# A fused two-layer network: dummy products moved to the front, GpSimd normalizing and rounding rows, and a new order of all steps

## The reference, cut to what matters

```
x = x + attn0(layernorm(x), ctx)        # 16 heads of 8, softmax
x = x + ffn0(layernorm(x))              # 8 experts of 512, one per row, gelu
x = x + attn1(layernorm(x), ctx)        # 16 query heads, 8 key heads
x = x + ffn1(layernorm(x))              # 15 experts of 128, top 3, and a shared one, relu
```

```
xn = x * rsqrt(mean(x*x) + 1e-6)
scale = 127 / max(max|xn|, 1e-5)
xq = clip(round(xn * scale), -128, 127) / scale
```

## Time and profile before

| | |
|---|---|
| times of three runs | 245.34, 240.26, 245.23 us (median 245.23) |
| profiled execution | 240.89 us, span 239.1 us |
| mean granted clock of TensorE | 0.971 |
| busy PE, DVE, ACT, POOL | 204.0, 174.3, 136.7, 76.7 us |

### The profile page before, as it was taken

How to read it: one execution, slowest core, us unless ns; L and a number is a source line. 1 busy time by engine, 2 the same in 40 slices (tenths; PEclk the granted TensorE clock), 3 DMA queues, 4 the chain that set the end, 5 groups by cost and what they waited for, 6 DMA issues and landing times.

```text
span 239.1 us, 5122 instructions
## 1 busy us (share of the span) xinstructions
PE 204.0 (85%) x1775; PEld 108.0 (45%) x1775; DVE 174.3 (73%) x500; ACT 136.7 (57%) x290; POOL 76.7 (32%) x162
## 2 busy tenths in 40 slices
PE   1687898799989999988478998899989698989994
PEld 1242253234343344567224474333343244889993
DVE  6979779976999566235726648988987832997774
ACT  2622137778849779340269566647777586544651
POOL 8889976992266600011200005400011010201000
PEclk9997589999999999999799999999999999999999
DMA  6152162494002100000003000850000000000000
GB/s 184 30 138 70 44 160 98 58 344 157 3 20 68 44 26 3 0 3 0 0 18 99 25 0 3 248 151 23 0 3 0 2 4 0 3 0 0 26 0 22
DMA packets 12810, 12.42 MB, mean 52 GB/s; under 512 B 2755, under 2 KB 11177, under 8 KB 12785
## 3 DMA queue, kind: packets, MB, share of 16 engines
q0 software_dynamic: 2528, 6.63, 9.8%
q1 hardware_dynamic: 8800, 4.95, 7.5%
q10 hardware_dynamic: 1456, 0.53, 0.9%
HBM read 7.84 MB, written 0.26 MB: 34 GB/s over the span
## 4 chain that ended last, share of the span: by engine, by line
PE 67%; DVE 14%; ACT 9%; issue 4%; DMA 2%; ACTq 1%; POOL 1%; SPq 1%; DVEq 0%; POOLq 0%
PE OB L1504 11%; PE SA L1472 8%; PE SB L1489 7%; ACT prob L836 6%; DVE mx L1086 5%; PE X L1624 3%; PE X L1606 3%; PE SA L1672 3%; PE X L1426 3%; PE X L1613 2%; DMA Q<-nm 2%; PE X L1513 2%; PE SB L1665 2%; PE X L1636 2%; PE SA L1665 2%
## 5 line engine op out<-in xcount | busy, mean ns | idle before, releaser
L1086 DVE TENSOR_REDUCE mx<-SA 128x1 bf16<-128x512 f32 x128 | 80.7, 683 | 14.7 <-PE SA L1472 13.9
L836 ACT ACTIVATE prob<-SB 128x512 f32<-128x512 f32 x128 | 69.4, 595 | 20.2 <-PE SB L1489 19.3
L640 POOL TENSOR_SCALAR vareps<-mv 128x2 f32<-128x2 f32 x10 | 1.9, 191 | 114.1 <-DVE mv L981 114.0
L1504 PE MATMUL OB<-prob,V 128*32 128x256 f32 x512 | 37.6, 387 | 0.3
L1489 PE MATMUL SB<-Q,K 64*128 64x256 bf16 x208 | 28.1, 274 | 3.3 <-ACT prob L836 1.5
L1472 PE MATMUL SA<-K,Q 64*128 64x512 bf16 x104 | 25.4, 388 | 4.3 <-DVE mx L1086 4.3
L1489 PEld LDWEIGHTS SB<-Q,K 64*128 64x128 bf16 x208 | 9.6, 94 | 23.7 <-ACT prob L836 15.6
L1504 PEld LDWEIGHTS OB<-prob,V 128*32 128x32 f32 x512 | 12.5, 108 | 14.1 <-issue 8.9
L1472 PEld LDWEIGHTS SA<-K,Q 64*128 64x128 bf16 x104 | 6.9, 94 | 17.1 <-DVE mx L1086 12.5
L887 ACT ACTIVATE wq<-w0s 128x1024 f32 x8 | 7.8, 1044 | 9.5 <-DVE eid L1238 9.3
L1313 DVE SCALAR_TENSOR_TENSOR acc<-SA,cw,acc 128x128 f32<-128x128 f32 x30 | 8.4, 345 | 1.6 <-PE SA L1672 1.6
(11 more groups left out here) (340 smaller groups left out, 400.2 us busy)
## 6 DMA issues: line engine op xcount, KB each, us to landing
w0s<-in_L_ffn_w_dram POOLq DMA_DIRECT2D x16, 256.0 KB, 4.5
wq<-in_L_ffn_eW_dram POOLq DMA_DIRECT2D x2, 960.0 KB, 7.2
K<-kp SPq DMA_DIRECT2D x12, 128.0 KB, 2.5
Q<-qp SPq DMA_DIRECT2D x18, 64.0 KB, 2.1
Q<-nm SPq DMA_DIRECT2D x50, 0.5 KB
K<-kp SPq DMA_DIRECT2D x12, 64.0 KB, 2.1
cx<-in_ctx_dram SPq DMA_DIRECT2D x2, 256.0 KB, 3.7
Q<-qp ACTq DMA_DIRECT2D x6, 64.0 KB, 2.1
```

The costliest lines, as they stand in the source:

```text
L836: act.activation(prob[:, g % 2, 2 * (i % 2) + a, 2 * u:2 * u + 2, :].rearrange("p k q -> p (k q)"), SB[n % NSB][:, :], ACT.Exp).then_inc(s ...
L1086: dve.tensor_reduce(mx[:, g % 2, i // 2, r, a:a + 1], SA[n % NSA][:, :], AX, ALU.max, negate=True).then_inc(s_sa_max, 1)
L1504: last = pe.matmul(OB[32 * j:32 * j + 32, 0:NQ], V[n][:, b, kt, first:first + 32], prob[:, gg % 2, j, kt, :], start=(kt == 0), stop=(kt == ...
```

## The change

Five things are done at once.

1. A new step `warm` makes two products of 256 columns out of the cleared tile `mx` into bank `OB`. Eight such steps stand at the start of TensorE's queue, two before the first scores. Of the 16 `unread` steps 12 are left.
2. `gnorm`: GpSimd normalizes the heads' output of batch 0 in layer 1 (6 operations on 128x128), in place of VectorE.
3. `round`: GpSimd rounds two of the four quantized tiles (batch 1 of `q1`, batch 0 of `o1`; 4 operations each). VectorE still works out the scales.
4. The casts of the second parts of keys and queries of batch 1, layer 0, go to ScalarE.
5. All steps stand in a new order. The sum over the weights of layer 1 is a step of its own (`w1_sum`).

```diff
+NORM_ON_GPSIMD = ('norm', 'o1', 0)
+ROUND_ON_GPSIMD = [('quant', 'q1', 1), ('quant', 'o1', 0)]
+CAST_ON_SCALAR = [('kproj', 0, 1), ('qproj', 0, 1)]
+SCHEDULE = [('warm', 0), ('zeros', 0), ('zeros', 1), ('warm', 1), ('warm', 2), ('warm', 3), ('stats', 'q0', 0),
...
+                elif kind == "gnorm":
+                    b = step[1]
+                    pool.wait_ge(in_gb, 48)
+                    pool.wait_ge(s_rstd, nth("stats", "o1", b))
+                    for r in range(R):
+                        last = pool.tensor_scalar(hn[:, b, r, :], stage_in["o1"][:, b, r, :], mv[:, b, r, 0:1], rstd[:, b, r:r + 1],
+                                                  ALU.subtract, ALU.mult)
+                    then(last)
+                    for r in range(R):
+                        last = pool.tensor_tensor(hn[:, b, r, :], hn[:, b, r, :], gamma_b[:, :], ALU.mult)
+                    then(last)
+                    for r in range(R):
+                        last = pool.tensor_tensor(hn[:, b, r, :], hn[:, b, r, :], beta_b[:, :], ALU.add)
+                    last.then_inc(s_gnorm, 1)
+                elif kind == "round":
+                    _, stage, b = step
+                    pool.wait_ge(s_scales, quantized_before("quant", stage, b))
+                    for r in range(R):
+                        last = pool.tensor_scalar(hn[:, b, r, :], hn[:, b, r, :], qs[:, b, r:r + 1], MAGIC, ALU.mult, ALU.add)
+                    then(last)
+                    for r in range(R):
+                        last = pool.tensor_scalar(hn[:, b, r, :], hn[:, b, r, :], -MAGIC, dq[:, b, r:r + 1], ALU.add, ALU.mult)
+                    last.then_inc(s_round, 1)
...
+                    if step in CAST_ON_SCALAR:
+                        act.wait_ge(*xread(*step))
+                        act.activation(kp[0:rows, part_buffer(step), 1, :], kr[0:rows, part_buffer(step), :], ACT.Copy).then_inc(s_kp[n][b], 1)
...
+                    if step == NORM_ON_GPSIMD:
+                        act.wait_ge(s_gnorm, 1)
+                    else:
+                        act.wait_ge(s_norm, normed_before(*step))
...
+                    if step == NORM_ON_GPSIMD:
+                        dve.wait_ge(s_gnorm, 1)
+                        then(dve.tensor_reduce(amax[:, b, :], hn[:, b, :, :], AX, ALU.max, apply_absolute_value=True))
+                        continue
...
+                    if step in ROUND_ON_GPSIMD:
+                        dve.scalar_tensor_tensor(qs[:, b, :], inv[:, :], 127.0, rms[:, b, :], ALU.mult, ALU.mult).then_inc(s_scales, 1)
+                        continue
...
+                elif kind == "warm":
+                    pe.wait_ge(s_mx, 1)
+                    for k in range(2):
+                        pe.matmul(OB[:, 0:NQ], mx[:, 0].rearrange("p x r c -> p (x r c)"), mx[:, :].rearrange("p g x r c -> p (g x r c)"),
+                                  start=True, stop=True)
```

More of the change, by code:

```diff
@@ L200, in nth, with normed_before, quantized_before @@
     return ORDER[step[0]].index(step) + 1
+def normed_before(*step):
+    return sum(s != NORM_ON_GPSIMD for s in ORDER["norm"][:nth(*step)])
+def quantized_before(*step):
+    return sum((s in ROUND_ON_GPSIMD) == (step in ROUND_ON_GPSIMD) for s in ORDER["quant"][:nth(*step)])
 def transformer(nc, x, ctx, Wq, bq, Wk, bk, Wv, bv, Wo, bo, w_red, wg, w1, b1, w2, b2, wq1, wk1, wv1, wo1,
@@ L253, in transformer @@
         inv = sb("inv", [P, R])
-        qs = sb("qs", [P, R])
-        dq = sb("dq", [P, R])
+        qs = sb("qs", [P, B, R])
+        dq = sb("dq", [P, B, R])
         cx = sb("cx", [P, B * KT, D])
@@ L806, in _ @@
                     last.then_inc(s_qp[n][b], 1)
+                    if step in CAST_ON_SCALAR:
+                        act.wait_ge(*xread(*step))
+                        act.activation(qp[:, part_buffer(step), 1, :], qr[:, part_buffer(step), :], ACT.Copy).then_inc(s_qp[n][b], 1)
                 elif kind == "kplace":
@@ L852, in _ @@
                     b = step[2]
-                    act.wait_ge(s_norm, nth(*step))
+                    if step == NORM_ON_GPSIMD:
+                        act.wait_ge(s_gnorm, 1)
+                    else:
+                        act.wait_ge(s_norm, normed_before(*step))
                     for r in range(R):
@@ L1006, in _ @@
                         continue
-                    dve.wait_ge(s_norm, nth(*step))
+                    dve.wait_ge(s_norm, normed_before(*step))
                     then(dve.tensor_reduce(amax[:, b, :], hn[:, b, :, :], AX, ALU.max, apply_absolute_value=True))
@@ L1015, in _ @@
                     then(dve.reciprocal(inv[:, :], mxn[:, :]))
-                    dve.tensor_scalar(dq[:, :], mxn[:, :], 1.0 / 127.0, None, ALU.mult)
-                    then(dve.scalar_tensor_tensor(qs[:, :], inv[:, :], 127.0, rms[:, b, :], ALU.mult, ALU.mult))
+                    dve.tensor_scalar(dq[:, b, :], mxn[:, :], 1.0 / 127.0, None, ALU.mult)
+                    if step in ROUND_ON_GPSIMD:
+                        dve.scalar_tensor_tensor(qs[:, b, :], inv[:, :], 127.0, rms[:, b, :], ALU.mult, ALU.mult).then_inc(s_scales, 1)
+                        continue
+                    then(dve.scalar_tensor_tensor(qs[:, b, :], inv[:, :], 127.0, rms[:, b, :], ALU.mult, ALU.mult))
                     for r in range(R):
-                        last = dve.tensor_scalar(hn[:, b, r, :], hn[:, b, r, :], qs[:, r:r + 1], MAGIC, ALU.mult, ALU.add)
+                        last = dve.tensor_scalar(hn[:, b, r, :], hn[:, b, r, :], qs[:, b, r:r + 1], MAGIC, ALU.mult, ALU.add)
                     then(last)
                     for r in range(R):
-                        last = dve.tensor_scalar(hn[:, b, r, :], hn[:, b, r, :], -MAGIC, dq[:, r:r + 1], ALU.add, ALU.mult)
+                        last = dve.tensor_scalar(hn[:, b, r, :], hn[:, b, r, :], -MAGIC, dq[:, b, r:r + 1], ALU.add, ALU.mult)
                     last.then_inc(s_quant, 1)
@@ L1071, in _ @@
                     last.then_inc(xdone(step), 1)
-                    dve.wait_ge(*xread(*step))
-                    dve.tensor_copy(parts[:, 1, :], rest).then_inc(done, 1)
+                    if step not in CAST_ON_SCALAR:
+                        dve.wait_ge(*xread(*step))
+                        dve.tensor_copy(parts[:, 1, :], rest).then_inc(done, 1)
                     dve.wait_ge(done, 2)
@@ L1115, in _ @@
                     dve.tensor_scalar(wgn[:, :], wgn[:, :], wgs[:, 2:3], None, ALU.mult).then_inc(s_wgn, 1)
-                elif kind == "w1_measure":
+                elif kind == "w1_sum":
                     dve.wait_ge(in_w1n, 64)
                     dve.tensor_reduce(wsum[:, :], w1n[:, :, :], AX, ALU.add, apply_absolute_value=True).then_inc(s_wabs, 1)
+                elif kind == "w1_measure":
                     dve.wait_ge(*xfull(step))
@@ L1520, in _ @@
                     else:
-                        pe.wait_ge(s_quant, nth("quant", "o1", b))
+                        pe.wait_ge(s_round if ("quant", "o1", b) in ROUND_ON_GPSIMD else s_quant, quantized_before("quant", "o1", b))
                     for r in range(R):
```

108 lines of the change are left out of this document (55 added, 53 removed), and 54 rows, old and new, of the table SCHEDULE.

## The result

The changed kernel took 245.88 us in the median of four runs (245.19 to 246.62), the kernel before 243.51 in the median of its four (240.26 to 245.34). The ratio is 1.020, with a 95% interval of 1.011 to 1.029. The forecast was 237.7 us, with 233 to 243 as its range; the change is slower by 1 to 2%. Every kernel here has some executions a few us longer at a lower clock (two of the four of the kernel before), and the ratios and the medians of the experiments leave those out.

A forecast was written before the change was run, and what follows sets the result against it. TensorE was taken as the bound (busy 204.0 of 239.1 us, 67% of the chain). From 240.9 us, -0.4 (front), -1.0 and -0.5 (unread products), -1.6 (VectorE's work) and +0.3 (GpSimd's chain) gave 237.7 us, range 233 to 243.

The forecast's parts named there:

- the sentence on the roundings: Roundings moved to GpSimd: 4 operations, 1.6 us, claimed to be covered by over 4 us of steps before their transposes.
- the second attention: Layer 1's attention: fewer unread products and less VectorE work, with GpSimd's slower chain against them; -2.3 us.
- between the layers: Middle of the kernel, where TensorE waits for VectorE: removing a copy or a faster gather brings nothing; 0, ends -1 and +1.
- the last network: End of the kernel: its only pair of unread products removed, all taken as on the path; -0.5 us.
- The front: Start to group 2's exponentials: first reduction at 19.4 (fast) or 21.1 us (slow); net -0.4 us, or +1.3 if slow.
- my third rival: Front: the 16 products end too early and the clock stays at 1.2 GHz past 31 us; 244.0 us, chance 0.12.
- VectorE's relief: Second layer: rounding and normalizing taken from VectorE, 3.6 us of work, half of TensorE's 3.3 us waits returning; -1.6 us.
- GpSimd's chain of six operations: Layer 1, batch 0 normalizing on GpSimd: 2.4 us after a power of 0.7, making ScalarE's squares wait; +0.3 us.
- Unread products: Two pairs dropped in the second attention, one in the last network, all taken as on the path; -1.0 and -0.5 us.
- Nothing of it is on the path: Rival: unread products stood in waits and VectorE's freed time lies idle, only the front counts; 240.5 us, chance 0.20.
- The signs: Trace marks named beforehand, such as first reduction near 19.4 us, clock above 0.9 in 24 to 30 us, VectorE busy 170.5 us.
- GpSimd holds VectorE: Rival: the 14 new GpSimd operations (5.8 us) block VectorE through the shared port, half on the path; 240.6 us, chance 0.06.

The follow-up runs named there:

- round_back: Changed kernel with the rounding of batch 1 of q1 back on VectorE, so the layer 1 weight load issues earlier; 242.7 us, ratio 1.012.
- load_late: Changed kernel with the load of layer 1's expert weights held until the first two maxima of group 13 are done; 241.7 us, ratio 1.003.
- late_max2: load_late with group 2's maxima transposed after the first quarter of group 3 and batch 1's query stacking one place earlier on SyncE's queue; 239.8 us, ratio 0.995.
- late_gap: load_late with GpSimd's fill of V moved later and 24 more products in TensorE's idle gap at the front; 239.8 us, ratio 0.999.
- combo: Changed kernel with the edits of load_late, late_gap and late_max2 together; 238.6 us (3 runs), ratio 0.995.
- combo_sync: combo with the layer 1 expert-weight load on SyncE's queue, issued after the first maximum of group 14; 238.2 us, ratio 0.988.
- after_again: The changed kernel unaltered, measured once more in five later runs; 246.5 us, ratio 1.010.
- no_warm: Changed kernel without its ten new steps of products on the cleared tile; 246.8 us, ratio 1.027.
- sync_unread: combo_sync with three pairs of unread products put back, two in the second attention and one in the last network; 238.9 us, ratio 0.993.
- fill_later: Changed kernel with GpSimd's fill of V moved behind the power of the context's deviation; 245.8 us, ratio 1.010.
- before_load_late: Kernel before with one added wait: layer 1's expert-weight load issues only when all maxima of group 10 are reduced; 245.0 us (2 runs).

## Why the prediction was wrong, point by point

- **The step that failed** is the sentence on the roundings: "The roundings (4 operations, 1.6 us) are covered by over 4 us of steps before their transposes." It is true of the transposes. I did not ask what else stood behind these operations on GpSimd's queue. It was the load of layer 1's weights, and behind that, by way of the shared transfer engines (busy share 1.01 in 156 to 162 us), group 10's maxima. It cost 3.8 to 4.8 us by the medians of round_back and load_late, and 4.1 us of the second attention (62.3 us against load_late's 58.2). I had the price in hand (a move of 4.59 us beside expert loads), but tied it to a slow front alone.
- **The account.** Against the forecast's span of 235.9 us (239.1 and the sum's -3.2) the trace had 244.9, 9.0 more. From the rows of both chains: layer 0 +1.2 where I had -0.4, between the layers -0.1 where I had 0, the second attention +4.1 where I had -2.3, the last network +0.6 where I had -0.5. The second attention's 6.4 us are 4.2 of idle time (TensorE was idle 2.9 us more than before, where I had 1.3 less; the stall alone is 4.08) and 2.2 of busy time (1.2 more, where I had 1.0 less). The clock accounts for the busy part: it was 0.72 in 162 to 168 us, behind the stall, 0.80 in 180 to 186 and 0.92 in 186 to 192 us, and 1.00 in 148 to 204 us before; late_max2, at 1.00 throughout, is busy for 49.8 us of this stretch, 1.4 less than the kernel before. With the load out of the way the stretch takes 57.0 to 58.2 us (load_late, late_gap, late_max2, combo, combo_sync) against 58.2 before, so of the 2.3 us that I had forecast for it 0 to 1.2 us came.
- **The front.** The sum gave 19.4 (fast) or 21.1 us (slow) for the first reduction and took the fast one; it came at 21.58, slow. The 0.5 us left are no more than the spread of such executions (20.98 to 21.89); the fill beside the normalizing, 0.68 us, was not in the sum. With a fast clock and the fill away it came at 19.84 to 20.02. From there to the end of group 2's transpose the prediction's terms add up to 22.7 us, not 22.4, and 23.0 were measured. The move of the maxima landed 5.1 us behind it, where the sum had 5.0. The six reductions of group 3 ahead of the joint transposes were in the sum; that they held TensorE (1.46 us in load_late, 0.30 in after_again) I did not see.
- **The reason for the slow front** was partly in my third rival: the 16 products end too early. What I did not see is that they make it worse, since without them these projections ran at full clock. The page "TensorE: Matmul & The Clock Gate" of the Trainium skill (Part 1, What's actually happening) has the slow state as the default and activity as the release; the rows of no_warm and of the changed kernel agree with it (unread pairs of 1.06 us at 8.40 us and 0.61 at 7.45). The rival's time of 244.0 us was near by luck, its mechanism (slow past 31 us, group 2 at 51.8) was not what happened: the clock was full from 17 to 36 us.
- **VectorE's relief** was put at -1.6 + 0.3 = -1.3 us; two pairs of kernels give -1.9 and -2.0. It was right in sign and 0.6 to 0.7 us too small. GpSimd's chain of six operations took 3.3 us, not the estimated 2.4; ScalarE waited 0.57 us for it at the squares, and the measured net includes that. The 14 new GpSimd operations took 6.3 us, where the prediction wrote 5.8 and its own terms (2.4 and twice 1.6) add up to 5.6.
- **Unread products**: -1.5 forecast; -0.7 by the medians and -1.2 by the ratios of sync_unread, neither clear of the spread, and nothing in the traces of the second attention. "Nothing of it is on the path" is wrong for VectorE's work and open for these.
- **The signs.** VectorE's busy time (169.7 us, 170.5 forecast), the clock in 24 to 30 us (1.00) and TensorE's idle time in 48 to 110 us (3.7 us, 3.4 before) came out as for a right forecast; the slow key projection, the first reduction and the idle time in the second attention as for a wrong one.
- **GpSimd holds VectorE** was right in kind and at a place I had not looked, a moved fill; the 14 new operations ran beside reductions.
- **Left open**: the last network took 39.5 us from the last values to the end, 38.8 before. That was not tried. How much of the 1.2 us of layer 0 is the slow projections' and how much chance is not shown either.

## What to carry to other kernels

When work moves to an engine with little to do, read that engine's queue behind the place: here the price was not the operation but the first thing queued after it, a large load, and what that load then ran into. Small transfers on the critical path should be kept apart from bulk loads by choosing when the load starts (after one move has landed, in the longest stretch before the next), not by issuing it as early as it can be. Products that are to keep the clock up should reach up to the work that needs it; with idle time behind them they put the fall of the clock right onto that work here.

## What the runs showed of the hardware

- A transfer of maxima (half a kilobyte each) took 2.06 us in combo_sync, where the load had all but ended, and 5.95 to 7.04 us beside the load of 2.1 MB, in five kernels that had the load there (the changed one, after_again, fill_later, no_warm, before_load_late).
- A GpSimd fill of 128x1336 float32 (1.22 us) stretched two VectorE operations of 128x128 from 0.60 to 1.28 us.
- TensorE can be at the slow level while it is fully busy: after the idle time of 8.06 to 10.65 us the granted clock was 0.50 in 12 to 16 us with 4.00 of 4 us busy.
- Products of 256 columns issued from 1.58 us took 0.22 us each while the clock column read 1.00; the same products from 7.87 us in late_gap took 0.12 us each. The column is no evidence for the first microseconds.
